# Softmax divisors spread by repeating loads instead of widening matmuls, and GpSimd's scatter moved to the head of its step

## Chip, cores and metric

The kernel runs on one core of a Trainium2 chip. The metric is the device time of one execution in microseconds, here the median of three. TensorE's clock has two levels, 1.2 and 2.4 GHz; a granted clock of 1.00 is the upper one and 0.50 the lower one.

## The reference, cut to what matters

Four sequences of 512 tokens with 512 channels go through a gated cross attention (32 query heads in 8 groups, 16 channels each, causal) and a gated mixture of experts:

```python
x = x + tanh(g_xattn[0]) * xattn(layernorm(x), ctx, ctx, mask, w_q, w_k, w_v, w_o, b_o)
x = x + tanh(g_ffn[0]) * ffn(layernorm(x), Wg, W1, W3, W2, Ws1, Ws3, Ws2)
```

Inside `xattn` each head's output is a softmax-weighted sum of values, divided by the sum of its weights, and all heads together are then projected with `w_o` and the bias `b_o`. Inside `ffn` a shared expert is applied to all tokens, and each token also goes to 4 of 16 experts, whose results are added with the router's weights.

## The kernel before

The kernel is five stages, each a block whose engines wait for each other at its end: `stage_project` (layer norm, queries, keys, values), `stage_attend`, `stage_close` (normalising the heads, output projection, residual, second layer norm, router scores), `stage_shared` (shared expert and routing tables) and `stage_experts` (79 tiles of 128 token slots).

**Attention** handles 32 items (a sequence and a group of four heads). For each it writes an unnormalised output of 128 rows to DRAM (`do`): each head has 16 channels and 16 copies of its softmax sum. SP's program (L586 to L606) is written out in order: loads for later items, the row of maxima, the store of the item before (L584), and in item 28 the loads of the sums of sequences 0 to 2 and of sequence 0's channels. ScalarE's copy of an item into `a_o` waits until the store before has landed. After the last maximum VectorE splits the bias into three bf16 parts (L656 to L671), and then takes the reciprocal of the 96 rows of sums (L674) and rounds it into a high and a low part (L676, L678).

**The closing stage** needs, for each channel and token, the inverse of that head's sum. It has one row per head. TensorE widens it with a selecting matrix `pick` (L977): two matmuls (high and low part) per quarter of the channels into the PSUM tiles `c_den`, and VectorE multiplies the channels by them (L931). The whole order of TensorE's work is in L1031 to L1054: 16 token tiles, four per sequence; for each a projection (`project`, one matmul for the bias at L985 and eight at L987 into a ring of RING = 3 banks), then the widening for the next sequence's quarter, and from the ninth tile on a transpose of a normalised tile (`turn`, L1000), eight tiles behind. VectorE does in each tile the scaled addition of the residual (L946), the statistics (L949) and then the multiply for the next sequence; after four tiles it finishes the deviation (L954, L115 to L127) and normalises (L963). A sequence's first projection waits until all four of its multiplies are done. SP loads the last sequence's sums, then the channels of sequence 1, the gate's scalar `gx`, the shared expert's weights and the channels of sequences 2 and 3. ScalarE takes the tanh of the scalar (L844), and the scaled additions wait for it. GpSimd subtracts high parts from the weights to get their low parts (L886, L890), and stores the normalised tokens.

**The experts.** In every tile TensorE makes gate and up products in three passes, turns the hidden row tile, multiplies down in three passes (L1706), and the third of these needs the low part of the hidden tile. GpSimd's step (L1587 to L1598) makes the low part of the tile before (`low_h`, L1582), the product of gate and up (L1593), then issues the scatter-add of the results two tiles back (L1577) and a gather four tiles ahead (L105). A scatter waits for ScalarE's result (L1624) and for the landing of the scatter before it. After the last tile GpSimd makes one more low part and issues the last two scatters.

Of the kernel before, what the change touches and what calls it, by code (L numbers as in the profile page):

```python
# [16 lines left out]
P = 128  # L17
# [125 lines left out]

def context(io, b):
# [80 lines left out]
def stage_project(nc, io, dram):  # L225

    SPIN, SEAM = 48, 48
    with ExitStack() as c:  # L228
# [15 lines left out]
        pick, less = sb("p_pick", [P, KD * P]), sb("p_less", [P, P])  # L244
# [60 lines left out]
        def _(eng):  # L305
            begin(eng, s_eps, s_ones, s_fill, s_mask, s_warm, io["s_pick"])
# [16 lines left out]
            eng.memset(pick[:], 0.0).then_inc(s_fill, 1)  # L323
# [7 lines left out]
            eng.wait_ge(s_fill, 6)  # L331
# [6 lines left out]
            eng.wait_ge(s_mask, BATCH + 4)  # L338
            eng.tensor_copy(io["lessr"], less[:]).then_inc(io["s_pick"], 1)
            eng.tensor_copy(io["pick"], pick[:]).then_inc(io["s_pick"], 1)  # L340
# [4 lines left out]
            eng.wait_ge(s_fill, 8)  # L345
# [174 lines left out]
def stage_attend(nc, io, dram):  # L520
# [3 lines left out]
    with ExitStack() as c:  # L524
# [45 lines left out]
        def _(eng):  # L570
# [15 lines left out]
            for i in range(NIT):  # L586
# [56 lines left out]
        def _(eng):  # L643
            begin(eng, s_split, io["s_triple"], io["s_inv"])
# [10 lines left out]

            eng.memset(three, 0.0).then_inc(s_split, 1)  # L656
# [15 lines left out]
            eng.wait_ge(io["s_sums"], 16)  # L672
            most = slice(0, (BATCH - 1) * GROUPS * HG)
            eng.reciprocal(inv[most], sums[most]).then_inc(s_split, 1)  # L674
            eng.wait_ge(s_split, 7)
# [91 lines left out]
def stage_close(nc, io, dram):  # L767
# [4 lines left out]
    with ExitStack() as c:  # L772
# [152 lines left out]
        def _(eng):  # L925
# [7 lines left out]
            for k in range(KD):  # L933
                normalise(0, k)
# [876 lines left out]
```

## Time and profile before

| what | us |
|---|---|
| median of 3 runs (lowest, highest) | 1240.26 (1237.85, 1240.94) |
| the profiled execution | 1240.24 |
| its span, first to last instruction | 1238.2 |
| TensorE busy, matmuls | 1199.9 (97%) |
| VectorE, ScalarE, GpSimd busy | 636.2, 576.4, 626.3 |
| closing stage, first matmul to end of the block | 359.9 to 461 |
| experts, about | 675 to the end |

Times inside the kernel are microseconds from the span's first instruction. In a timeline row the first number is the start, the second the length; several instructions in a row are merged ("x4"), and the bracket tells how long the engine had been idle and what ended that. The profiled execution's time lies 2.0 us above its span, which is what lies around the instructions.

### The profile page before, as it was taken

What the parts mean: (1) busy time and instruction counts of PE and PEld (TensorE: products, weight loads), DVE (VectorE), ACT (ScalarE), POOL (GpSimd) and SP (SyncE); (2) the same over time, 40 slices, a digit from 0 to 9 for tenths busy, and PEclk for the clock granted to TensorE, in tenths of its full rate; (3) what the DMA queues carried; (4) which work ended last, traced back from release to release, by engine and by line L of the source; (5) the groups of instructions that cost most, each with busy time, mean ns of one, the idle gap of its engine ahead of it and who ended that gap; (6) DMA issues with size and microseconds to landing.
All of it is one profiled execution on the core that took longest, in us unless ns stands there. A gap on an engine that the chain in (4) does not pass through costs nothing. (4 is left out here: it accounts for less than half of the span.)

```text
span 1238.2 us, 23635 instructions
## 1 busy us (share of the span) xinstructions
PE 1199.9 (97%) x7811; PEld 919.4 (74%) x7812; DVE 636.2 (51%) x1832; ACT 576.4 (47%) x990; POOL 626.3 (51%) x662
## 2 busy tenths in 40 slices
PE   7999999999999989999998999999999999999994
PEld 5564555555543458888887999999999999999994
DVE  5337999999965658865142133322523444542100
ACT  1221777777742234322332554555554554555552
POOL 7010333433334124635562666666666667767663
PEclk8999999999989999999999999999999999999997
DMA  9462544444545050100133455665655666665433
GB/s 348 149 189 99 154 125 131 126 135 126 145 134 155 30 204 17 52 35 35 51 121 113 107 102 144 142 150 138 155 138 129 163 147 146 142 150 138 83 61 42
DMA packets 73965, 153.27 MB, mean 124 GB/s; under 512 B 10740, under 2 KB 16372, under 8 KB 73128
## 3 DMA queue, kind: packets, MB, share of 16 engines
q1 hardware_dynamic: 52856, 102.50, 25.6%
q0 software_dynamic: 21040, 49.88, 19.5%
q8 instruction: 41, 0.67, 0.2%
q14 instruction: 28, 0.23, 0.1%
HBM read 97.69 MB, written 52.23 MB: 121 GB/s over the span
## 5 line engine op out<-in xcount | busy, mean ns | idle before, releaser
L1553 DVE CAST e_w<-e_w 128x480 fp32r<-128x480 f32 x135 | 75.7, 561 | 303.9 <-DMA e_w<-in_w2T 299.7
L653 DVE CUSTOM_DVE_ANT_0 a_mb<-a_mb,late 128x512 f32<-128x512 f32 (+1 forms) x480 | 217.3, 527 | 6.3 <-PE a_mb L696 4.6
L1706 PE MATMUL e_yps<-e_w,e_hT 128*128 x711 | 197.2, 404 | 0.9 <-ACT e_hT L1616 0.9
L639 ACT ACTIVATE a_at<-a_eb 128x1024 f32<-128x1024 f32 (+1 forms) x192 | 163.4, 869 | 38.5 <-PE a_eb L717 25.7
L566 POOL TENSOR_SCALAR_AFFINE_SELECT a_at<-a_at 128x256 f32<-128x256 f32 (+1 forms) x192 | 94.2, 491 | 170.6 <-ACT a_at L639 170.6
L1685 PE MATMUL e_up<-e_w,e_xT 128*128 x948 | 170.4, 328 | 0.0
L1685 PE MATMUL e_gate<-e_w,e_xT 128*128 x948 | 169.2, 327 | 1.0 <-issue 1.0
L1685 PEld LDWEIGHTS e_gate<-e_w,e_xT 128*128 128x128 f32 x948 | 157.2, 190 | 11.4 <-issue 6.6
L1685 PEld LDWEIGHTS e_up<-e_w,e_xT 128*128 128x128 f32 x948 | 149.4, 188 | 0.0
L1706 PEld LDWEIGHTS e_yps<-e_w,e_hT 128*128 128x128 f32 x711 | 128.1, 189 | 25.4 <-issue 1.2
L1577 POOL DMA_INDIRECT out<-e_y,scatter x79 | 128.3, 1625 | 25.3 <-issue 14.1
L1582 POOL TENSOR_TENSOR e_hT<-e_hc,e_hT 128x384 fp32r<-128x384 f32 x79 | 85.6, 1083 | 108.4 <-ACT e_hc L1617 108.4
L696 PE MATMUL a_mb<-a_k,a_q 49*128 49x512 f32 (+1 forms) x480 | 132.4, 373 | 0.8 <-PEq L228 0.8
L696 PEld LDWEIGHTS a_mb<-a_k,a_q 49*128 49x128 f32 x480 | 74.2, 184 | 65.5 <-DVE a_mx L653 39.2
L1560 DVE TENSOR_TENSOR e_w<-e_w 128x480 fp32r<-128x480 f32 x135 | 101.6, 753 | 4.7
L740 PE MATMUL a_pv<-a_at,a_v 128*32 128x128 f32 (+1 forms) x1792 | 102.2, 327 | 0.2
L1593 POOL TENSOR_TENSOR e_h<-e_act,e_upc 128x352 f32<-128x352 f32 x79 | 79.5, 1006 | 38.4 <-ACT e_upc L1635 37.3
L105 POOL DMA_INDIRECT e_x<-dx,gather x79 | 82.6, 1046 | 23.6 <-issue 23.5
L1612 ACT ACTIVATE e_xT<-e_xps 128x512 fp32r<-128x512 f32 x79 | 47.2, 597 | 81.5 <-PE e_xps L1676 76.3
L717 PE MATMUL a_eb<-a_q,a_k 50*128 50x512 f32 (+1 forms) x256 | 84.1, 420 | 0.1
L1631 ACT ACTIVATE e_act<-e_gate 128x352 f32<-128x352 f32 x79 | 36.7, 464 | 95.8 <-PE e_gate L1685 95.8
L1635 ACT ACTIVATE e_upc<-e_up 128x352 f32<-128x352 f32 x79 | 36.8, 466 | 79.0 <-PE e_up L1685 79.0
(265 smaller groups left out, 1873.7 us busy)
## 6 DMA issues: line engine op xcount, KB each, us to landing
e_w<-in_w13T SPq DMA_DIRECT2D x16, 1408.0 KB
dq<-p_parts SPq DMA_DIRECT2D x32, 256.0 KB, 2.4
a_q<-dq SPq DMA_DIRECT2D x64, 128.0 KB
do<-a_o SPq DMA_DIRECT2D x32, 256.0 KB, 2.3
e_w<-in_w2T SPq DMA_DIRECT2D x16, 512.0 KB
a_k<-dk SPq DMA_DIRECT2D x64, 98.0 KB
e_w<-in_ctxT SPq DMA_DIRECT2D x4, 1024.0 KB, 14.1
e_w<-in_x SPq DMA_DIRECT2D x4, 1024.0 KB, 13.5
```

The lines of the kernel that those rows point to most:

```text
L105: eng.indirect_dma_start(out=io["rows"][n], out_offset=None, in_=dram["x2"], in_offset=bass.IndirectOffsetOnAxis(ap=io["gather"][:, g:g + ...
L566: eng.affine_select(out=square, in_=square, compare_op=ALU.is_ge, fill=0.0, base=0, pattern=[[0, 2 * len(js)], [1, P]], channel_multiplier ...
L639: eng.activation(to, scores, ACT.Exp, scale=0.25).then_inc(s_exp, 1)
L653: eng.tensor_tensor_reduce(out=b[:, 0:w], in0=b[:, 0:w], in1=io["late"][:, SEQ - w:SEQ], scale=1.0, scalar=3 * NEG, op0=ALU.add, op1=ALU.m ...
L696: mm = eng.matmul(b, q[r][rows, j, ch * P:(ch + 1) * P], k[r][rows, 0:b.shape[-1]], start=True, stop=True)
L717: return eng.matmul(eb[u % 2][:, t, n0:SEQ], keys, q[r][rows, js[0], n0:SEQ], start=True, stop=True)
L740: mm = eng.matmul(pv[32 * h:32 * h + 32, cols], v[of % NB][:, ch, :], at[of % 2][:, ch, 2 * j + t, cols], start=ch == 0 and n0 == 0, stop= ...
L1560: eng.tensor_tensor(w[rows, r, rest], w[rows, r, rest].bitcast(F32), w[rows, r, cols].bitcast(F32), ALU.subtract).then_inc(s_low, 1)
L1577: eng.indirect_dma_start(out=out, out_offset=bass.IndirectOffsetOnAxis(ap=io["scatter"][:, g:g + 1], axis=0), in_=y[n][:], in_offset=None, ...
L1582: eng.tensor_tensor(hT[r][:, 1], hc[:], hT[r][:, 0].bitcast(F32), ALU.subtract).then_inc(s_hlow, 1)
L1685: mm = eng.matmul(out[r][:], xT[r][:, mine, k, :], w[:, bass.ds(buf, 1), its * SIDE + at:its * SIDE + at + INTER].rearrange("p b n -> p (b ...
L1706: mm = eng.matmul(yps[:], hT[r][0:size, mine, n, :], w[0:size, bass.ds(buf, 1), its * SIDE + at:its * SIDE + at + D].rearrange("p b n -> p ...
```

## The change

The divisors are no longer widened on TensorE. VectorE's reciprocal of the first three sequences is taken straight after the last maximum; SP stores it to a DRAM tensor `dinv`, one DMA per sequence, in the last item but one, and in the last item waits for these stores and loads sequence 0's rows back, repeated over the 16 channels of every head (1 MB to 128 partitions). VectorE's four multiplies for sequence 0 move into the attention block. In the closing stage SP loads the scalar first, then the channels of sequence 1 and its repeated inverse, and so on; the last sequence's inverse makes its trip to DRAM in that stage, and its repeated rows come in two pieces. Both operands of the multiply now lie in SBUF. The multiply for the next sequence comes first in VectorE's tile instead of last; the ring of banks has five members. The matrix `pick` and the high and low parts of the inverse are gone. In the experts the scatter moves to the head of GpSimd's step, and the last tile's low part is made by VectorE straight from PSUM.

```diff
+def store_inverse(eng, dram, b, tile, done):
+    heads = tile[b * GROUPS * HG:(b + 1) * GROUPS * HG]
+    eng.dma_start(dram["inv"][b].rearrange("r (k n) -> k r n", k=KD), heads).then_inc(done, 16)
+
+def load_inverse(eng, dram, b, k0, k1, tile, done):
+    src = dram["inv"][b:b + 1, :, k0 * SEQ:k1 * SEQ].broadcast_to([HD, 2 * HG, (k1 - k0) * SEQ])
+    eng.dma_start(tile.rearrange("p k n -> p (k n)"), src).then_inc(done, 16)
+
+def normalise(eng, io, o, inv, k):
+    eng.tensor_tensor(o[:, k], o[:, k], inv, ALU.mult).then_inc(io["s_on"], 1)
...
@@ stage_project, gpsimd @@
-            for b in range(BATCH):
-                mine = pick[b * GROUPS * HG:(b + 1) * GROUPS * HG].rearrange("p (k w h) -> p k w h", k=KD, w=HD)
-                eng.affine_select(out=mine, in_=mine, compare_op=ALU.not_equal, fill=1.0, base=0,
-                                  pattern=[[-2 * HG, KD], [0, HD], [-1, 2 * HG]], channel_multiplier=1).then_inc(s_mask, 1)
...
@@ stage_attend, sync @@
+                if i == NIT - 1:
+                    eng.wait_ge(io["s_sums"], 16 * BATCH)
+                    load_inverse(eng, dram, 0, 0, KD, io["inv"], io["s_heads"])
                 if i:
                     store(i - 1)
...
+                if i == NIT - 2:
+                    eng.wait_ge(io["s_inv"], 2)
+                    for b in range(BATCH - 1):
+                        store_inverse(eng, dram, b, inv, io["s_sums"])
@@ stage_attend, vector @@
+            most = slice(0, (BATCH - 1) * GROUPS * HG)
+            eng.wait_ge(io["s_sums"], 16)
+            eng.reciprocal(inv[most], sums[most]).then_inc(io["s_inv"], 1)
             eng.memset(three, 0.0).then_inc(s_split, 1)
...
-            eng.tensor_copy(io["inv"][most, 0], inv[most]).then_inc(io["s_inv"], 1)
-            eng.wait_ge(io["s_inv"], 2)
-            eng.tensor_tensor(io["inv"][most, 1], inv[most], io["inv"][most, 0].bitcast(F32), ALU.subtract).then_inc(io["s_inv"], 1)
+            eng.wait_ge(io["s_heads"], 16 * (KD + 1))
+            for n in range(KD):
+                normalise(eng, io, io["heads"], io["inv"][:, n], n)
@@ stage_close, sync @@
-    RING, LAG, SEAM = 3, 8, 24
+    RING, LAG, SEAM = 5, 8, 24
...
+            eng.dma_start(gx[:], io["gx"].broadcast_to([P, 1])).then_inc(s_g, 16)
+            load_heads(eng, dram, 1, o[1], s_o[1])
+            load_inverse(eng, dram, 1, 0, KD, x2[0][:], s_o[1])
             load_sums(eng, dram, BATCH - 1, BATCH, sums, io["s_sums"])
...
             for b in range(2, BATCH):
                 load_heads(eng, dram, b, o[b], s_o[b])
+            load_inverse(eng, dram, 2, 0, KD, x2[1][:], s_o[2])
+            eng.wait_ge(io["s_inv"], 3)
+            store_inverse(eng, dram, BATCH - 1, inv, io["s_sums"])
+            eng.wait_ge(io["s_sums"], 16 * (BATCH + 2))
+            load_inverse(eng, dram, BATCH - 1, 0, KD - 1, rest[:], s_o[BATCH - 1])
...
@@ stage_close, vector @@
+                    if b + 1 < BATCH:
+                        divide(b + 1, j)
+                    if i == 1:
+                        eng.wait_ge(io["s_sums"], 16 * (BATCH + 1))
+                        eng.reciprocal(inv[LAST], sums[LAST]).then_inc(io["s_inv"], 1)
                     eng.wait_ge(s_op, i + 2)
...
                     eng.bn_stats(stats[:, j, :], x1[b][:, j]).then_inc(s_st, 1)
-                    if b + 1 < BATCH:
-                        normalise(b + 1, j)
@@ stage_close, tensor @@
-            for k in range(KD):
-                widen(0, k)
...
                     project(b, j)
-                    if b + 1 < BATCH:
-                        widen(b + 1, j)
@@ stage_experts, gpsimd @@
+                if g >= 2:
+                    scatter(g - 2)
                 if g:
                     low_h(g - 1, 1 - r)
...
-                if g >= 2:
-                    scatter(g - 2)
...
-            low_h(LAST, LAST % 2)
             scatter(LAST - 1)
             scatter(LAST)
@@ stage_experts, vector @@
+            high, rest = hT[LAST % 2][:, 0], hT[LAST % 2][:, 1]
+            eng.wait_ge(s_hT, 2 * LAST + 2)
+            eng.tensor_tensor(rest, hps[:], high.bitcast(F32), ALU.subtract).then_inc(s_hlow, 1)
@@ stage_experts, scalar @@
-                eng.activation(hc[:], hps[:], ACT.Copy).then_inc(s_hT, 1)
+                if not isinstance(g, int) or g < LAST:
+                    eng.activation(hc[:], hps[:], ACT.Copy).then_inc(s_hT, 1)
```

## Rows read from the trace of the kernel before

**Rows 1.** Timeline, end of attention and head of the closing stage
```profile
343.13 0.11 DVE L656 MEMSET k_three<- 96x64 uint32 x1
...
346.88 9.90 SPq L584 DMA_DIRECT2D do<-a_o  x3
...
359.87 1.16 PE L977 MATMUL c_den<-k_inv,k_pick 32*128 32x512 f32 x4 [1.20 <-PEq L524]
...
364.12 3.35 DVE L936 RECIPROCAL e_w<-e_w 32x512 f32<-32x512 f32 x1
...
364.24 0.59 PE L985 MATMUL c_op<-k_triple,k_three 96*128 96x512 bf16 x1 [0.87 <-DVE e_w L931]
...
367.37 0.20 ACT L844 ACTIVATE c_tg<-c_gx 128x1 f32<-128x1 f32 x1 [10.93 <-DMA c_gx<-in_gx]
...
371.02 0.69 DVE L949 BATCH_NORM_STATS2 c_stats<-e_w 128x6 f32<-128x512 f32 x1
```

**Rows 2.** Timeline, first matmul of sequences 1 to 3, last scaled addition
```profile
385.51 0.61 PE L985 MATMUL c_op<-k_triple,k_three 96*128 96x512 bf16 x1 [1.51 <-DVE c_o L931]
...
406.40 0.39 PE L985 MATMUL c_op<-k_triple,k_three 96*128 96x512 bf16 x1 [1.50 <-DVE c_o L931]
...
427.08 0.39 PE L985 MATMUL c_op<-k_triple,k_three 96*128 96x512 bf16 x1 [0.91 <-DVE c_o L931]
...
445.12 0.75 DVE L946 SCALAR_TENSOR_TENSOR e_w<-c_op,c_tg,e_w 128x512 f32<-128x512 f32 x1 [2.17 <-PE c_op L987]
```

**Rows 3.** Timeline, steps of one token tile with and without widening
```profile
395.34 0.73 PE L977 MATMUL c_den<-k_inv,k_pick 32*128 32x512 f32 x2
...
399.75 0.73 PE L977 MATMUL c_den<-k_inv,k_pick 32*128 32x512 f32 x2
...
437.18 0.38 PE L985 MATMUL c_op<-k_triple,k_three 96*128 96x512 bf16 x1
...
441.27 0.38 PE L985 MATMUL c_op<-k_triple,k_three 96*128 96x512 bf16 x1
```

**Rows 4.** Timeline, the last scatters and the last result but one
```profile
1219.34 1.58 POOL L1577 DMA_INDIRECT out<-e_y,scatter  x1 [0.15 <-issue]
...
1219.81 0.69 ACT L1624 ACTIVATE e_y<-e_yps,scale 128x512 f32<-128x512 f32 x1 [1.63 <-PE e_yps L1706]
...
1224.73 1.56 POOL L1577 DMA_INDIRECT out<-e_y,scatter  x1 [2.38 <-ACT e_y L1624]
1230.29 1.56 POOL L1577 DMA_INDIRECT out<-e_y,scatter  x1 [4.00 <-DMA out<-e_y,scatter]
```

**Rows 5.** DMA issues of the span: size of one, median us to landing
```profile
do<-a_o SPq DMA_DIRECT2D x32, 256.0 KB, 2.3
...
out<-e_y,scatter POOLq DMA_INDIRECT x79, 4.9
...
e_w<-in_bo SPq DMA_DIRECT2D x1, 256.0 KB, 3.6
```

**Rows 6.** Windows: PE, PEld, DVE, ACT, POOL busy (count), granted clock, DMA share, GB/s
```profile
127.00:128.00 1.00, 1.00 (x12) 0.46 (x11) 0.76 (x3) 0.79 (x1) 0.15 (x1) 1.00 0.87 240
...
386.00:387.00 1.00, 1.00 (x3) 0.48 (x2) 0.82 (x7) 0.07 (x1) 0.00 (x0) 0.50 1.03 387
```

**Rows 7.** Lines L931 and L1560 (min/median/max ns), and timeline of L963
```profile
L931 DVE TENSOR_TENSOR c_o<-c_o,c_den x12: 669/670/672, 371.6 to 426.4; 128x512 f32<-128x512 f32 x12
...
L1560 DVE TENSOR_TENSOR e_w<-e_w x135: 657/659/1434, 675.2 to 1149.1; 128x480 fp32r<-128x480 f32 x120, 96x512 fp32r<-96x512 f32 x15
...
432.15 6.66 DVE L963 TENSOR_SCALAR c_x<-e_w,c_mv,c_rstd 128x512 f32<-128x512 f32 x4
```

**Rows 8.** Timeline, one tile of the experts on GpSimd, ScalarE and TensorE
```profile
897.79 1.06 POOL L1593 TENSOR_TENSOR e_h<-e_act,e_upc 128x352 f32<-128x352 f32 x1 [0.26 <-ACT e_upc L1635]
...
900.10 0.69 ACT L1624 ACTIVATE e_y<-e_yps,scale 128x512 f32<-128x512 f32 x1 [0.18 <-PE e_yps L1706]
...
903.25 1.01 POOL L1582 TENSOR_TENSOR e_hT<-e_hc,e_hT 128x384 fp32r<-128x384 f32 x1 [1.35 <-ACT e_hc L1617]
...
905.84 0.64 PEld L1706 LDWEIGHTS e_yps<-e_w,e_hT 128*128 128x128 f32 x3
```

More of the change, by code:

```diff
@@ L243, in stage_project @@
         const = sb("p_const", [1, 2, SEQ])
-        pick, less = sb("p_pick", [P, KD * P]), sb("p_less", [P, P])
+        less = sb("p_less", [P, P])
         proj = [ps(f"p_proj{i}", [P, SEQ]) for i in range(KD + 1)]
@@ L789, in stage_close @@
         wraw = sb("c_wraw", [P, GATE])
+        assert GATE - UP == SEQ
         stats, mv, rstd = sb("c_stats", [P, CH, 6]), sb("c_mv", [P, CH, 2]), sb("c_rstd", [P, CH])
         root, work, eps = sb("c_root", [P, CH]), sb("c_work", [P, CH]), sb("c_eps", [P, 1])
-        den = [ps(f"c_den{i}", [P, SEQ]) for i in range(2)]
+        rest = sb("c_inv", [P, KD - 1, SEQ])
         op = [ps(f"c_op{i}", [P, D]) for i in range(RING)]
@@ L800, in stage_close @@
         s_tg, s_eps = sem("c_stg"), sem("c_seps")
-        s_den, s_on, s_op, s_x1, s_st, s_mv, s_root, s_newton, s_x2 = (
-            sem(f"c_s{n}") for n in ("den", "on", "op", "x1", "st", "mv", "root", "newton", "x2"))
+        s_op, s_x1, s_st, s_mv, s_root, s_newton, s_x2 = (
+            sem(f"c_s{n}") for n in ("op", "x1", "st", "mv", "root", "newton", "x2"))
         s_tr, s_xT, s_lg, s_lc, s_whigh, s_wlow = (sem(f"c_s{n}") for n in ("tr", "xT", "lg", "lc", "whigh", "wlow"))
@@ L805, in stage_close @@
         weights = shared_weights(io)
+        spread = [None, [x2[0][:, n] for n in range(KD)], [x2[1][:, n] for n in range(KD)], [rest[:, n] for n in range(KD - 1)] + [wraw[:, UP:]]]
         block = c.enter_context(nc.Block())
@@ L925, in _, with divide @@
         def _(eng):
[L926 to L927 removed]
+            begin(eng, s_x1, s_st, s_mv, s_newton, s_x2)
+            def divide(b, k):
                 if k == 0:
[L929 to L940 removed]
+                    eng.wait_ge(s_o[b], 16 * (KD + (1 if b < BATCH - 1 else 2)))
+                normalise(eng, io, o[b], spread[b][k], k)
             eng.wait_ge(s_tg, 2)
@@ L967, in _ @@
         def _(eng):
-            begin(eng, s_den, s_op, s_tr, s_lg, s_part)
-            def widen(b, k):
-                d = b * KD + k
-                if d >= 2:
-                    eng.wait_ge(s_on, d)
-                rows = slice(b * GROUPS * HG, (b + 1) * GROUPS * HG)
-                if b == BATCH - 1 and k == 0:
-                    eng.wait_ge(io["s_inv"], 6)
-                for part in range(2):
-                    mm = eng.matmul(den[k % 2][:], io["pick"][rows, k * P:(k + 1) * P], io["inv"][rows, part], start=part == 0, stop=part == 1)
-                mm.then_inc(s_den, 1)
+            begin(eng, s_op, s_tr, s_lg, s_part)
             def project(b, j):
                 i = b * CH + j
-                eng.wait_ge(s_on, (b + 1) * KD + 1)
+                eng.wait_ge(io["s_on"], (b + 1) * KD + 1)
                 if i >= RING:
@@ L1029, in score @@
                     mm.then_inc(s_lg, 1)
-            eng.wait_ge(io["s_pick"], 3)
-            eng.wait_ge(io["s_inv"], 3)
-            for k in range(KD):
-                widen(0, k)
             eng.wait_ge(io["s_wo"], 16 * (KD + 2))
@@ L1051, in _ @@
                     score(BATCH - 1, i - (NT + LAG - CH + 2))
-            eng.wait_ge(s_on, BATCH * KD + 1)
+            eng.wait_ge(s_x1, NT + 1)
             for _ in range(SEAM):
-                eng.matmul(den[0][:, 0:P], io["onesb"], io["before"], start=True, stop=True)
+                eng.matmul(op[0][:, 0:P], io["onesb"], io["before"], start=True, stop=True)
 def stage_shared(nc, io, dram, out):
```

37 lines of the change are left out of this document (9 added, 28 removed).

## The prediction

> **What bounds the kernel now.** I read the page first: TensorE is busy nearly throughout, so time is gained only where it waits or does work that can go. The chain of waits ends in the experts' matmuls and, at the very end, in scatters. The timeline at the seam of attention and closing stage [rows 1] then shows four widening matmuls at 359.87, VectorE multiplying their results, and TensorE's first projection only at 364.24. The start of each later batch [rows 2] shows TensorE waiting for VectorE's multiply: 1.51 us at 385.51, 1.50 at 406.40, 0.91 at 427.08; a batch takes 20.9, 20.7 and 18.0 us (the last has no widening beside it). A step of one token tile [rows 3] takes 4.41 us with its two widening matmuls (0.73), and 4.09 without them but with a turn (437.18 to 441.27). So TensorE bounds this stage, with VectorE close behind. At the kernel's end [rows 4] the last scatters follow each other at 5.4 and 5.6 us (1219.34, 1224.73, 1230.29), though the result of the last tile but one is ready at 1220.5: each scatter waits for the one before to land (the row of 1224.73 names ScalarE's result, but that had been there for 4 us).
>
> **Attention's end.** The reciprocal of three batches' sums moves up to 343.1, straight behind the last maximum, and takes 3.35 us (by the row at 364.12, of as many columns), so it is done when SP has put the store of 346.88 in its queue [rows 1]. The bias's split slides behind it and is hidden: TensorE needs it at 360. The two rounding operations go too; they were hidden. SP then issues three stores of the inverse (1.5 us), waits for them, and loads 1 MB that repeats rows. A store lands 2.3 us after its issue [rows 5]. What a load that repeats rows costs, the trace shows only for the bias, one row over 128 partitions: 240 GB/s at a DMA share of 0.87, or 276 at full share; plain loads move 387 [rows 6]. I take 276 as the nearest kind: 3.8 us for 1 MB. The bounds are 2.7 us (387 GB/s) and, if all of the bias load's 3.6 us from issue to landing [rows 5] was transfer, 4 x 3.6 = 14.4. So the store lands at 350.7, the load at 350.7 + 3.8 + 1.6 = 356.1 (the 1.6 is a store's 2.3 less its own movement), and four multiplies of 0.67 end at 358.8. Behind SP's wait are the stores of the last two head groups; the last but one now queues behind 1 MB, and ScalarE's last copy waits for its landing. I charge 0.5 us for both to the block's end.
>
> **First batch of the closing stage.** The eight widening matmuls at its head are gone and the projections start at 360.4, but that gain isn't kept: VectorE's new first work is the multiply of batch 1, which waits for 1 MB of heads and 1 MB of inverse. Heads and the gate's scalar, in the old order, have landed at 367.37 [rows 1]; in the new order the same two come the other way round. Add 0.5 and 3.8: 371.7. Then VectorE does four multiplies (0.67), three scaled additions (0.75, row 445.12) and three statistics (0.69), and the last batch's reciprocal (3.35; SP, and so the last inverse, waits on it): 2.7 + 2.2 + 2.1 + 3.4 = 10.4, and 0.6 for the port (below). Batch 1 starts at 382.7 instead of 385.5: **2.8 us**. TensorE is through its four tiles by 377 and waits. The five banks in place of three are worth next to nothing here: three tiles last until 373.2, and the first scaled addition frees a bank at 373.1. Loading the scalar first is costed at nothing, since tanh at 367.37 is hidden behind the projection, which ends at 370.
>
> **Batch 1.** Today: four steps of 4.41, the end wait of 1.50, and 20.89 - 17.64 - 1.50 = 1.75 us more because the clock is at its lower level after the wait (0.50 at 386 [rows 6]). The wait remains and so does, I assume, the slow start. New: 4 x 3.68 + 1.75 = 16.5. **4.4 us**. The end wait goes because each multiply now stands ahead of its step, not behind it. **Batch 2:** 20.69 becomes 4 x 4.09 = 16.4: **4.3 us**. **Batch 3** is as it was, less 0.5 us that I charge for VectorE being late with its four multiplies: its second normalisation meets GpSimd's weights. The last batch's divisors should be there: 9 MB queued from 359.4 at 276 GB/s end at 393, the store and reload of 64 KB and its piece make about 397, and they are wanted at 406. Sum for the stage: 2.8 + 4.4 + 4.3 - 0.5 = **11.0 us**. What follows, to the stage's end, hangs on the last projection as now.
>
> **The port.** Sixteen multiplies now read both operands from SBUF. With one from PSUM they took 669 to 672 ns whatever GpSimd did; the experts' subtraction with both in SBUF takes 657 ns but up to 1434, and at 432.15 four normalisations took 6.66 us beside GpSimd's splitting [rows 7]. The Trainium skill, "SBUF — State Buffer", section "Who interferes with whom", says a VectorE instruction with two SBUF inputs contends with a GpSimd one that reads SBUF, which speaks against this change; these rows agree. In the sum stand 0.6 us in batch 0 and 0.5 in batch 3.
>
> **Experts.** Scatter(g-2) goes from the end of GpSimd's step to its head. In a step [rows 8] the product before ends at 898.85, the gather that follows it 1.3 later at 900.15, its result is there at 900.79, so the scatter runs to about 902.5, ahead of the low part's 903.25. TensorE wants that part only at 905.84, 1.6 us after its end. So nothing per tile; 2.3 us is the slack before a tile gets longer. At the end the scatter of the last tile but two starts 5 us earlier and has landed by 1220, so the next starts at 1220.6 when its result is ready, and the last at about 1226.1 instead of 1230.29 (a landing is 4.9 [rows 5], 5.5 between two here): **4.2 us**. The last low part on VectorE and ScalarE's copy saved are worth nothing: the chain is the landings. The mask that selected channels goes from GpSimd's first microseconds, hidden under the input loads: nothing.
>
> **Sum.** 11.0 + 4.2 = 15.2. The profiled execution took 1240.24 us around a span of 1238.2, and the median is 1240.26: 1225.0 us. A measurement of this kernel tells 0.3% (3.7 us) from no change.
>
> **Rivals.**
> *Loads at half rate or less.* For: 16 copies of the same rows are read at once; no row shows it. Against: the bias row. At 7.6 us per MB the seam and batch 1's start lose 3.8 each and batch 2 some more: 1233. Chance 0.12.
> *The port decides.* If every multiply beside GpSimd waits a whole splitting operation (6.66 / 4 - 0.54 = 1.1 us more each), two in batch 0 and four in batch 3 lie on the path: 6.6 in place of 1.1, so 1230. The skill's rule would give this time. Against: GpSimd splits weights only in some stretches. Chance 0.13.
> *Better than forecast.* The load runs at 387 GB/s twice (2.2 us), the clock stays up through the wait (1.75), VectorE isn't late (1.1): 1220. For: after the waits at 406.40 and 427.08 the bias's matmul took 0.39 us, against 0.61 at 385.51 [rows 2]. Chance 0.15.
> *Slower than before.* Repeated rows come at a rate that makes the four loads the bound. All four lie ahead of batch 3, which at 3.8 us per MB could start at 397 + 6.7 = 403.7 for all that the loads demand (6.7: four multiplies with three steps between), and later by 4 x (L - 3.8) for L us per MB; with the scatter's 4.2 it breaks even at L = 10.7 and is over 0.3% slower from 11.6. At 14.4 it is 1255. Chance 0.03.
> *The scatter at the head holds the step.* If the previous scatter lands over 2.3 us late, TensorE waits in each of 77 tiles; 0.2 us each eats the whole gain: 1240. Against: a landing takes 4.9 of 7 us. Chance 0.03.
> The forecast itself has 0.54. Faster 0.94, same 0.03, slower 0.03. The range takes the better case's 1219 and goes up to 1232.
>
> **What would show it.** No widening; first projection near 360.4; VectorE's first multiply of the stage ending a wait for a load at 371 to 372; batch starts near 383, 399, 416; the last scaled addition near 434 instead of 445.12; last scatter near its predecessor plus 5.5, both 4 us nearer to the last result. It is wrong if the block of attention closes over 2 us later, if batch 2 or 3 waits for a load, or if a tile of the experts takes longer than now.

## The result and the profile after

The changed kernel took 1230.77 us in the median of 4 runs (1229.68 to 1231.72), the kernel before 1240.60 beside it (4 runs, 1237.85 to 1241.05): a ratio of 0.9929, with a 95% interval of 0.9910 to 0.9947. That is 9.8 us less, where 15.2 had been forecast; the direction and the range were right, the size was not. The profiled execution has a span of 1227.9 us against 1238.2.

Six distances between landmarks show where the time went. They are differences of starts in the timelines, for two profiles of each kernel (the second ones are the runs e12 and e11 below):

| from, to | before | before, again | after | after, again |
|---|---|---|---|---|
| attention's first matmul (from the span's start) | 119.33 | 119.22 | 118.34 | 118.36 |
| to the closing stage's first matmul | 240.54 | 240.60 | 243.16 | 243.46 |
| attention's first matmul to the last scaled addition | 325.79 | 325.87 | 317.53 | 317.58 |
| last scaled addition to the experts' first matmul | 221.28 | 223.84 | 225.51 | 225.44 |
| that to ScalarE's last result `e_y` | 557.02 | 557.17 | 556.59 | 556.72 |
| last `e_y` to the last scatter | 6.87 | 7.02 | 2.44 | 2.96 |

So attention and closing stage together gave 8.3 us, the scatters 4.1 to 4.4, and between them the span loses 1.6 to 4.2 us in a part that the change hardly touches. The experts' tiles are 0.4 us shorter in sum. The 1.0 us ahead of attention came with a shorter stretch at the lower clock in the first stage (19.0 to 26.5 us in place of 16.5 to 27.5, read in windows of half a microsecond). It is not the change's own: attention starts at 118.79 in e1 below, which has the first stage of the kernel before, and at 119.60 and 119.19 in e2 and e7, which have that of the changed kernel.

**The seam.** SP's queue at the end of attention, in the timeline of the changed kernel:

```profile
346.27 1.94 SPq L147 DMA_DIRECT2D dinv<-a_inv  x3
350.15 0.57 SPq L153 DMA_DIRECT2D e_w<-dinv  x1
351.41 7.20 SPq L594 DMA_DIRECT2D do<-a_o  x2
...
360.73 0.34 SPq L828 DMA_DIRECT2D c_gx<-in_gx  x1
```

the first of SP's loads in the next stage in the kernel before,

```profile
358.94 0.32 SPq L141 DMA_DIRECT2D e_w<-do  x1
```

and what VectorE and ScalarE do in the changed kernel:

```profile
357.00 2.49 DVE L158 TENSOR_TENSOR e_w<-e_w 128x512 f32<-128x512 f32 x4 [6.37 <-DMA e_w<-dinv]
...
357.66 0.60 ACT L637 ACTIVATE a_o<-a_pv 128x512 f32<-128x512 f32 x1 [4.17 <-DMA do<-a_o]
...
374.02 0.69 DVE L158 TENSOR_TENSOR c_o<-c_o,c_x 128x512 f32<-128x512 f32 x1 [14.52 <-DMA c_x<-dinv]
...
376.73 3.35 DVE L965 RECIPROCAL e_w<-e_w 32x512 f32<-32x512 f32 x1
...
383.48 0.94 DVE L158 TENSOR_TENSOR c_o<-c_o,c_x 128x512 f32<-128x512 f32 x1
```

The megabyte of repeated rows is issued at 350.15 and VectorE goes on at 357.00: 6.8 us, where I had 5.4. The store of the last item but one (351.41) stands in the same queue behind it, and ScalarE's last copy waits 4.17 us for its landing. The last store goes out only then, and SP is in the next stage at 360.73, where the kernel before had been at 358.94. With the 1.0 us from ahead of attention that is 2.8 us late (3.1 in e11 against e12); I had charged 0.5. The store did not wait in idle queues: in windows of half a microsecond the DMA engines move 1.33 MB between 351.5 and 357.0, which is the megabyte and the 256 KB of the store together, and nothing in the 2 us behind.

**The batches.** The starts of sequences 0 to 3 on TensorE, and the last scaled addition, which answer to [rows 1, 2]:

```profile
361.50 0.59 PE L993 MATMUL c_op<-k_triple,k_three 96*128 96x512 bf16 x1 [3.83 <-PEq L534]
...
384.48 0.61 PE L993 MATMUL c_op<-k_triple,k_three 96*128 96x512 bf16 x1 [5.30 <-DVE c_o L158]
...
400.77 0.38 PE L993 MATMUL c_op<-k_triple,k_three 96*128 96x512 bf16 x1
...
417.83 0.39 PE L993 MATMUL c_op<-k_triple,k_three 96*128 96x512 bf16 x1 [0.54 <-DVE c_o L158]
...
435.87 0.75 DVE L967 SCALAR_TENSOR_TENSOR e_w<-c_op,c_tg,e_w 128x512 f32<-128x512 f32 x1 [1.80 <-PE c_op L995]
```

Batch 1 starts 1.03 us earlier than before (nearly all of it the shift from ahead of attention), lasts 16.29 us in place of 20.89, batch 2 lasts 17.06 in place of 20.68, batch 3 18.04 as before. 1.03 + 4.60 + 3.62 = 9.25 us.

**The tail of the stage** is where time was lost again. TensorE's last scores, the matmuls at the seam and the first of the shared expert, changed kernel:

```profile
447.52 3.50 PE L1035 MATMUL c_lp<-e_w 128*128 128x16 f32 x24
450.86 2.72 PE L1056 MATMUL c_op<-before,onesb 128*128 128x128 bf16 x24
455.06 7.85 PE L1405 MATMUL s_gate<-s_xT,s_ws 128*128 x24 [1.48 <-issue]
```

and the same three in the kernel before:

```profile
456.77 2.75 PE L1027 MATMUL c_lp<-e_w 128*128 128x16 f32 x24
459.37 1.50 PE L1054 MATMUL c_den<-before,onesb 128*128 128x128 bf16 x24
462.27 5.73 PE L1403 MATMUL s_gate<-s_xT,s_ws 128*128 x24 [1.39 <-issue]
```

The work is the same; 0.75 + 1.22 + 2.12 = 4.1 us of difference. The windows of the changed kernel (columns as in [rows 6]) show the granted clock at its lower level there:

```profile
446.00:449.00 3.00, 3.00 (x29) 2.87 (x27) 0.00 (x0) 1.21 (x3) 0.00 (x0) 1.00 0.87 362
449.00:452.00 3.00, 3.00 (x24) 3.00 (x24) 0.00 (x0) 0.22 (x1) 0.00 (x0) 0.55 0.85 341
452.00:455.00 3.00, 1.58 (x15) 1.31 (x13) 0.06 (x1) 0.62 (x1) 0.65 (x5) 0.50 0.04 14
455.00:458.00 3.00, 2.94 (x7) 2.37 (x8) 2.21 (x10) 1.75 (x4) 0.00 (x0) 0.50 0.03 3
```

That of the kernel before is 1.00 throughout:

```profile
445.00:470.00 25.00, 21.02 (x159) 17.09 (x158) 12.11 (x49) 12.51 (x23) 4.09 (x10) 1.00 0.53 211
```

**The end of the kernel**, which answers to [rows 4]:

```profile
1211.33 1.01 POOL L1587 TENSOR_TENSOR e_hT<-e_hc,e_hT 128x384 fp32r<-128x384 f32 x1 [0.71 <-ACT e_hc L1622]
...
1215.31 1.56 POOL L1582 DMA_INDIRECT out<-e_y,scatter  x1 [1.58 <-ACT e_y L1629]
...
1217.97 0.69 ACT L1629 ACTIVATE e_y<-e_yps,scale 128x512 f32<-128x512 f32 x1 [2.56 <-PE e_yps L1711]
...
1220.41 1.57 POOL L1582 DMA_INDIRECT out<-e_y,scatter  x1 [3.54 <-DMA out<-e_y,scatter]
```

The last scatter but one goes out as soon as its result is there, and the last follows it by 5.1 us: it waits for the landing.

### The profile page after: what moved, and what is told of

Read it like the earlier page. It is cut to its first block and busy times, and to the rows that moved or that the text cites. A ratio compares the mean times of both kernels' runs of the same rounds, so it can differ in the third digit from the quotient of the medians.

```text
span 1227.9 us, 23555 instructions
## 1 busy us (share of the span) xinstructions
PE 1190.7 (97%) x7779; PEld 917.2 (75%) x7780; DVE 631.8 (51%) x1829; ACT 576.0 (47%) x989; POOL 618.1 (50%) x655
## 5 line engine op out<-in xcount | busy, mean ns | idle before, releaser
L1555 DVE CAST e_w<-e_w 128x480 fp32r<-128x480 f32 x135 | 71.5, 530 | 304.9 <-DMA e_w<-in_w2T 300.8
L1600 POOL TENSOR_TENSOR e_h<-e_act,e_upc 128x352 f32<-128x352 f32 x79 | 76.3, 966 | 39.7 <-ACT e_upc L1640 39.5
```

## The experiments

Twelve kernels ran. Those of one group shared a chip and the runs of the kernel before: e1 to e4 (13 runs of the kernel before, 1241.30 us in the median), e5 to e8 (21 runs, 1241.12) and e9 to e12 (13 runs, 1240.52). Since the chips differ, variants are compared by their ratio to the kernel before; that of the change is 0.9929 in its first comparison and 0.9936 in e11.

**e1, the scatter at the head alone**, in the kernel before, with the last low part left on GpSimd:

```diff
@@ kernel before, stage_experts, gpsimd @@
+                if g >= 2:
+                    scatter(g - 2)
                 if g:
                     low_h(g - 1, 1 - r)
...
-                if g >= 2:
-                    scatter(g - 2)
```

> The kernel before with nothing but the scatter moved to the head of GpSimd's step; the last low part stays on GpSimd. Theory A (landings chain the last scatters; order inside a tile costs nothing): all of the end's gain comes from this one move, the last scatter starts about 2.4 us behind the last result instead of 6.9, 1240.6 - 4.4 = 1236.2 us, and a tile stays at 6.98 us. Rival B (the low part on VectorE and the copy saved carry part of it, or tiles get longer at the head's wait): gain under 2.5 us, 1238 or more.

1238.32 us (10 runs), ratio 0.9974 (0.9959 to 0.9989). GpSimd at the end:

```profile
1223.22 1.01 POOL L1582 TENSOR_TENSOR e_hT<-e_hc,e_hT 128x384 fp32r<-128x384 f32 x1 [2.15 <-ACT e_hc L1617]
1224.39 1.56 POOL L1577 DMA_INDIRECT out<-e_y,scatter  x1 [0.16 <-issue]
1229.97 1.57 POOL L1577 DMA_INDIRECT out<-e_y,scatter  x1 [4.02 <-DMA out<-e_y,scatter]
```

The result of the last tile but one is there at 1222.39, and its scatter goes out at 1224.39: it stands behind the last low part on GpSimd, which waited 2.15 us for ScalarE. The last scatter comes 4.64 us behind the last result: 2.2 of the 6.87 are gone, not 4.2. The other 2.2 (4.64 against 2.44) is then the last low part's move to VectorE, with the copy that it saves ScalarE, which I had called worth nothing; no kernel with that move alone was run. No tile became longer (experts 556.96 us against 557.02).

**e2, the closing stage's part alone** (the changed kernel with the experts' edits undone: scatter behind the product, last low part on GpSimd, ScalarE's last copy back).

```diff
@@ changed kernel, stage_experts, gpsimd @@
-                if g >= 2:
-                    scatter(g - 2)
                 if g:
                     low_h(g - 1, 1 - r)
...
+                if g >= 2:
+                    scatter(g - 2)
...
+            low_h(LAST, LAST % 2)
             scatter(LAST - 1)
             scatter(LAST)
```

> The changed kernel with the experts' part of the kernel before (scatter behind the product, last low part on GpSimd). Theory A: the divisors' part alone is worth 1240.6 - 1230.8 - 4.4 = 5.4 us, so 1235.2 us. Rival B (the two parts do not add up, because what happens after the closing stage depends on when it ends): 1233 or less, or 1237 or more.

1233.33 us (1233.03 to 1235.87), ratio 0.9937 (0.9920 to 0.9954), between theory A's 1235.2 and rival B's 1233. The last scatter is again 6.49 us behind the last result, the stretch from attention to the last scaled addition 317.96. So the two halves are about 8 and 3 us on the medians; their sum, 11, is within what these medians leave open of the 9.8. The tail, from the last scaled addition to the experts, was 225.46 us here, as in both profiles of the whole change.

**e3, what the repetition costs.** The loads of the inverse read 8 KB rows of the tokens, as many bytes to the same places; the output is not the reference's.

```diff
@@ load_inverse @@
-    src = dram["inv"][b:b + 1, :, k0 * SEQ:k1 * SEQ].broadcast_to([HD, 2 * HG, (k1 - k0) * SEQ])
+    src = dram["plain"][b * SEQ:(b + 1) * SEQ].rearrange("(p a) d -> p (a d)", p=P)[:, k0 * SEQ:k1 * SEQ]
```

> The changed kernel, but each load of the repeated inverse reads as many bytes of the input tokens, one contiguous row of 8 KB per partition; so the division by the softmax sums is replaced by a product with tokens, and the routing is another. Only the closing stage is compared. Theory A (reading the same rows sixteen times costs transfer time): the first load lands in 5.4 us or less after its issue instead of 6.8, attention's block closes 1 to 1.5 us earlier, and batch 1 starts at 381 to 382 instead of 384.5. Rival B (a megabyte behind stores and heads takes this long whatever it reads): 6.8 within 0.3, batch 1 at 384 to 385.

1223.44 us in the one run. Theory A holds in its direction (batch 1 at 381.36), with a first load of 5.8 us where it said 5.4 or less. The landing times of the changed kernel's loads (issue to landing is the last column):

```profile
c_x<-dinv SPq DMA_DIRECT2D x2, 1024.0 KB, 13.6
e_w<-dinv SPq DMA_DIRECT2D x1, 1024.0 KB, 6.8
c_inv<-dinv SPq DMA_DIRECT2D x1, 768.0 KB, 5.6
```

and in e3 the same loads, with VectorE's first multiply and TensorE's batch 1:

```profile
c_x<-in_x SPq DMA_DIRECT2D x2, 1024.0 KB, 11.3
c_inv<-in_x SPq DMA_DIRECT2D x1, 768.0 KB, 4.5
```

```profile
356.26 2.50 DVE L158 TENSOR_TENSOR e_w<-e_w 128x512 f32<-128x512 f32 x4 [5.31 <-DMA e_w<-in_x]
...
381.36 0.39 PE L993 MATMUL c_op<-k_triple,k_three 96*128 96x512 bf16 x1 [2.67 <-DVE c_o L158]
```

Repeated rows cost 1.0 to 1.1 us per load more than plain ones of the same size (6.8 against 5.8, 5.6 against 4.5), and 2.3 in the median of the two that share the queue with the channels. The edit changes two things at once, the repetition and the tensor that is read (rows stored a few microseconds ago against input); which of them costs is not separated. Attention's first matmul lies 0.3 us later here. Batch 1 starts 3.1 us earlier, its first matmul takes 0.39 us and no longer 0.61, and the stretch to the last scaled addition is 312.85 in place of 317.53. So of the 4.7 us that the repeated loads cost 3.4 lie ahead of batch 1 (262.75 from attention's first matmul against 266.14) and the other 1.3 are about what the lower clock cost in that batch, which in e3 stays away (16.29 us in the changed kernel, 14.6 for four steps of 3.65). All this rests on one run.

**e4, more work for TensorE in the tail**: six matmuls of 128 columns, written to a spare bank, behind each of the last four scores.

```diff
@@ stage_close, tensor @@
                     score(BATCH - 1, i - (NT + LAG - CH + 2))
+                    for _ in range(FILL):
+                        eng.matmul(op[1][:, 0:P], io["onesb"], io["before"], start=True, stop=True)
```

> The changed kernel with six 128-column bf16 matmuls into a free bank after each of the last four groups of score matmuls, 24 in all, about 1.4 us of TensorE. Theory A (the lower clock level that the changed kernel has from 449.3 to 459.2 came because TensorE did little in the last score matmuls of 16 columns, and it costs 4.2 us): the granted clock stays at 1.00 over the seam, 1230.8 - 4.2 + 1.4 = 1228 us. Rival B (the drop comes whatever TensorE does there): the clock still falls and the time is 1232.

1227.92 us (1226.77 to 1230.68), ratio 0.9900 (0.9879 to 0.9921). The lower level is there for about 3.5 us, from 450.2, and not for 10 (449.2 to 459.5):

```profile
449.00:452.00 3.00, 3.00 (x36) 3.00 (x34) 0.00 (x0) 0.22 (x1) 0.00 (x0) 0.71 0.62 254
452.00:455.00 3.00, 1.61 (x12) 1.26 (x11) 0.60 (x4) 1.27 (x1) 0.65 (x5) 0.72 0.03 3
455.00:458.00 3.00, 3.00 (x15) 2.46 (x14) 2.28 (x8) 1.74 (x4) 0.00 (x0) 1.00 0.01 0
```

From the last scaled addition to the experts it took 223.82 us in place of 225.5. Of the 2.3 us by which this profile's span is shorter than that of the change, 0.8 lie ahead of attention and 1.2 in attention, which the edit does not touch, so the lead does not show what the edit is worth. Theory A's time came, but not its reason in full: the clock still falls. Its interval overlaps that of the change itself (0.9910 to 0.9947); e10 puts the same matmuls to a second test.

**e5, the last sequence's reciprocal later**, ahead of the fourth scaled addition and not the second, so that batch 1's multiplies do not stand behind it.

```diff
@@ stage_close, vector @@
-                    if i == 1:
+                    if i == CH - 1:
                         eng.wait_ge(io["s_sums"], 16 * (BATCH + 1))
```

> The changed kernel with the last sequence's reciprocal (3.35 us) moved in VectorE's program from behind the second multiply for batch 1 to behind the fourth. Theory A (VectorE's chain of four multiplies, three additions, three statistics and this reciprocal sets the start of batch 1, and the last inverse has 6 us of slack, since its store queues behind loads until 388 in any case): batch 1 starts 3.3 us earlier, at 381.1 instead of 384.5, and the kernel takes 1230.8 - 3.3 = 1227.5 us. Rival B (the last inverse is as late as batch 1): batch 1 starts earlier but batch 3 waits for its divisors, and the time stays within 1 us.

1235.85 us (11 runs), ratio 0.9958 (0.9943 to 0.9974): by the ratios some 3 us slower than the changed kernel. Batch 1 started at 380.26, 4.2 us earlier, as meant, and with a wait of 0.88. But batch 3 began at 422.08. VectorE and GpSimd in e5, and TensorE's start of batch 3:

```profile
403.79 0.18 DVE L115 RECIPROCAL c_rstd<-c_root 128x4 f32<-128x4 f32 x1 [4.57 <-ACT c_root L873]
...
416.98 4.50 POOL L925 TENSOR_TENSOR s_xT<-c_x2T,s_xT 128x2048 fp32r<-128x2048 f32 x1 [5.32 <-ACT s_xT L892]
417.74 4.28 DVE L158 TENSOR_TENSOR c_o<-c_o,c_wraw 128x512 f32<-128x512 f32 x1
...
422.08 0.61 PE L993 MATMUL c_op<-k_triple,k_three 96*128 96x512 bf16 x1 [6.38 <-DVE c_o L158]
```

VectorE, early now, waits 4.57 us for a square root that ScalarE has queued behind rounding weights still on their way (they land at 400.7). And its fourth multiply of batch 2 meets GpSimd's 4.50 us subtraction, which had started 0.76 us earlier: 4.28 us in place of 0.67. The Trainium skill, "SBUF — State Buffer", section "Who interferes with whom", says that a VectorE instruction with two SBUF inputs contends with a GpSimd one that reads SBUF, and that the port pair they share is an exclusive lock. These rows agree: the multiply ends 0.54 us behind the subtraction (422.02 against 421.48), about its own length of 0.67. The changed kernel itself escaped this by little: there the fourth multiply starts at 417.10 and GpSimd's subtraction at 418.57.

**e6, sequence 0's inverse with a semaphore of its own**, stored and loaded ahead of the stores of the other two.

```diff
@@ stage_attend, sync @@
-                if i == NIT - 1:
-                    eng.wait_ge(io["s_sums"], 16 * BATCH)
-                    load_inverse(eng, dram, 0, 0, KD, io["inv"], io["s_heads"])
...
-                    for b in range(BATCH - 1):
-                        store_inverse(eng, dram, b, inv, io["s_sums"])
+                    store_inverse(eng, dram, 0, inv, io["s_first"])
+                    eng.wait_ge(io["s_first"], 16)
+                    load_inverse(eng, dram, 0, 0, KD, io["inv"], io["s_heads"])
+                    for b in range(1, BATCH - 1):
+                        store_inverse(eng, dram, b, inv, io["s_sums"])
...
```

> The changed kernel, but sequence 0's inverse is stored first with a semaphore of its own, and its repeated rows are loaded as soon as that one store has landed, before the other two stores are issued. Theory A (the close of attention's block is late because the megabyte of repeated rows lies in the queues ahead of the store of the last group but one, whose landing ScalarE's last copy waits for): the load is issued 1.3 us earlier, the block closes 1.3 us earlier, 1229.5 us. Rival B (the first batch of the closing stage waits for the landing of its own two megabytes and the time hidden there returns): the block closes earlier and batch 1 starts no more than 0.3 us earlier.

1231.21 us (1228.84 to 1238.18), ratio 0.9928 (0.9902 to 0.9954): nothing. The multiply came at 356.68, 1.0 us nearer to attention's start, but the closing stage still began 243.30 us behind it (243.16 and 243.46 without the edit). So VectorE's multiplies do not close the block; the last stores do, of which ScalarE's copy waits for the first to land:

```profile
352.20 7.16 SPq L594 DMA_DIRECT2D do<-a_o  x2
...
358.41 0.60 ACT L638 ACTIVATE a_o<-a_pv 128x512 f32<-128x512 f32 x1 [4.12 <-DMA do<-a_o]
```

But theory A failed too. The megabyte is issued 1.2 us nearer to attention's start, and the store behind it, issued when its data is there as before, still takes 6.2 us to the copy (358.41 against 352.20; 6.25 in the changed kernel, 5.4 in e3; the median store of this kernel lands in 2.3 [rows 5]). So what holds the store is the traffic that it meets, and an earlier start of the load does not shorten it; why is not shown. In the profiled execution the port collision of e5 happened here too (4.86 us for the fourth multiply, beside a subtraction of 4.49 that started 0.19 us earlier), and batch 3 waited 6.38 us.

**e7, the multiply behind its step again**, as it was before the change:

```diff
@@ stage_close, vector @@
-                    if b + 1 < BATCH:
-                        divide(b + 1, j)
...
                     eng.bn_stats(stats[:, j, :], x1[b][:, j]).then_inc(s_st, 1)
+                    if b + 1 < BATCH:
+                        divide(b + 1, j)
```

> The changed kernel with VectorE's multiply for the next sequence behind the statistics of its tile, as in the kernel before. Theory A (the head of the step is what removes TensorE's waits at batches 2 and 3): the waits of 1.5 us at the starts of batches 2 and 3 return, batch 1 starts about where it does now or up to 1 us later, 1230.8 + 3 = 1233.8 us. Rival B (with five banks TensorE's lead hides it): within 1 us of 1230.8.

1234.40 us (9 runs), ratio 0.9953 (0.9933 to 0.9974): by the ratios 2 to 3 us slower than the change, and 3.1 in the profile (320.67 us from attention's first matmul to the last scaled addition, in place of 317.53). The waits are back, against none and 0.54 us:

```profile
403.56 0.39 PE L993 MATMUL c_op<-k_triple,k_three 96*128 96x512 bf16 x1 [2.17 <-DVE c_o L158]
...
421.82 0.39 PE L993 MATMUL c_op<-k_triple,k_three 96*128 96x512 bf16 x1 [1.73 <-DVE c_o L158]
```

**e8, three banks and the gate's scalar behind the inverse**, as in the old order:

```diff
@@ stage_close @@
-    RING, LAG, SEAM = 5, 8, 24
+    RING, LAG, SEAM = 3, 8, 24
...
-            eng.dma_start(gx[:], io["gx"].broadcast_to([P, 1])).then_inc(s_g, 16)
             load_heads(eng, dram, 1, o[1], s_o[1])
             load_inverse(eng, dram, 1, 0, KD, x2[0][:], s_o[1])
             load_sums(eng, dram, BATCH - 1, BATCH, sums, io["s_sums"])
+            eng.dma_start(gx[:], io["gx"].broadcast_to([P, 1])).then_inc(s_g, 16)
```

> The changed kernel with three banks instead of five and the gate's scalar loaded behind the channels and the inverse of sequence 1. Theory A (neither is worth anything: the first scaled addition waits for the megabyte of inverse in any case): within 1 us of 1230.8. Rival B (with three banks TensorE stops for the fourth tile until the first addition, and again while VectorE takes the reciprocal; or tanh comes behind the multiply): 1232 or more, the fourth projection starting after 375 instead of 375.4 or the first addition after 375.

1227.84 us (1225.46 to 1232.83), ratio 0.9908 (0.9880 to 0.9935), below what either theory gave. Neither edit is worth anything; that they cost something is not shown, since the intervals overlap and of this profile's lead of 4.2 us 1.5 lie ahead of attention and 1.4 in it, which the edit does not touch. From the closing stage's first matmul to the last scaled addition it took 73.96 us, against 74.37 and 74.12 in the two profiles of the change.

**e9 and e10, a version meant to beat the change**: e5's later reciprocal, ScalarE's second square root ahead of rounding the shared down projection, and GpSimd's subtraction held until the multiplies are done; e10 with e4's matmuls as well.

```diff
@@ on top of e5: stage_close, scalar and gpsimd @@
             deviation(0)
+            deviation(1)
             high_weights(2)
...
-                if b + 1 < BATCH:
+                if 0 < b and b + 1 < BATCH:
                     deviation(b + 1)
...
                     eng.wait_ge(s_xhigh, CH + 1)
+                    eng.wait_ge(io["s_on"], BATCH * KD + 1)
                     eng.tensor_tensor(xT[:, 1], x2T[0], xT[:, 0].bitcast(F32), ALU.subtract).then_inc(s_wlow, 1)
```

> The changed kernel with three edits: VectorE takes the last sequence's reciprocal ahead of the fourth scaled addition, not the second (as in the run e5); ScalarE takes the second batch's square root ahead of rounding the experts' shared down projection, which waits for a load; and GpSimd's subtraction of the first batch's transposed operand (4.5 us, two SBUF operands) waits until VectorE has done all its multiplies. Theory A (what spoiled e5 was VectorE's 4.57 us wait for that square root and the 4.28 us multiply beside GpSimd's subtraction; both go here): batch 1 starts near 380.5, no multiply of batch 3 takes over 1.5 us, batch 3 starts near 414 with a wait under 1.5 us in place of 6.38, last scaled addition near 432; median near 1227.5 (1225 to 1230). Rival B (VectorE's own work between the batches is what is late): batch 3 still waits 3 us or more though every multiply takes 0.7 us, last addition 435 or later, 1230 or more.

> As e9, with e4's 24 extra matmuls of 128 columns among the last scores (they write a spare bank and change no value). Theory A (the gains add: e4 gave 2.9 us on the median of the changed kernel, through a shorter stretch at the lower clock in the tail): 1225 (1222 to 1228), and the lower level at the seam to the shared stage lasts under 7 us. Rival B (the lower level comes elsewhere then, or is as long whatever the tail does): within 1 us of e9, with 10 us at the lower level after the last projection.

e9 took 1233.01 us (ratio 0.9927, 0.9910 to 0.9944), e10 1232.74 (0.9947, 0.9924 to 0.9970), the changed kernel beside them 1232.23. No gain. In e9 batch 1 starts at 381.12, and the wait for the square root is 0.36 us; but batch 3 waits 4.08:

```profile
403.58 6.73 POOL L912 TENSOR_TENSOR e_w<-e_w 128x512 fp32r<-128x512 f32 x5 [14.63 <-ACT e_w L865]
...
404.26 0.48 DVE L979 MEMSET e_w<- 64x512 f32 x1 [2.10 <-ACT e_w L866]
404.78 5.82 DVE L984 TENSOR_SCALAR c_x<-e_w,c_mv,c_rstd 128x512 f32<-128x512 f32 x4
410.52 1.75 DVE L158 TENSOR_TENSOR c_o<-c_o,c_inv 128x512 f32<-128x512 f32 x1
...
418.27 0.39 PE L995 MATMUL c_op<-k_triple,k_three 96*128 96x512 bf16 x1 [4.08 <-DVE c_o L158]
```

VectorE's next instruction, clearing the padding rows of those weights, waits 2.10 us for the same rounding; then four normalisations take 5.82 us beside GpSimd's splitting, where the first batch's took 1.91, and the multiply behind them 1.75. So the normalisation behind batch 1 is tied to when the down projection arrives (ScalarE's rounding starts on its landing, at 400.04 in the changed kernel, 400.71 in e5 and 401.17 in e9): an earlier batch 1 only waits there. Theory A had named one of the two waits on that load, and rival B's forecast of the wait (3 us or more) came, though not its condition that every multiply takes 0.7 us. In e10 the tail was at the lower level from 448.4 to 458.6 in spite of the extra matmuls, and they then took time themselves (227.48 us from the last scaled addition to the experts, 227.07 in e9 without them): e4's short stretch does not repeat.

**e11 and e12, both kernels again**, for a second profile of each.

> The changed kernel again, unchanged, as the baseline of e9 and e10 on the same chip and as a second profile of it. Theory A (the lower clock of 449 to 460 in the first profile is usual for this kernel, since two of the variants with the same tail showed it): median 1230.8 within 1 us, a stretch of 7 us or more at the lower level between the last projection and the shared stage's matmuls, shared stage's matmuls over 6 us for the first 36. Rival B (it was that execution's own): no such stretch, profiled span under 1225.

> The kernel before again, unchanged, for a second profile of it. Theory A (the kernel before has in most executions no stretch at the lower level in the tail, which is why the change gave 4 us back there): span near 1238, the shared stage's first matmul 17.1 to 17.3 us behind the last scaled addition and no stretch between 445 and 475. Rival B (where such stretches fall differs between executions of either kernel alike): a stretch of 3 to 10 us in the tail here as well, and then about 1240 to 1242 in the span.

e11: 1232.23 us (1227.83 to 1237.61), ratio 0.9936 (0.9911 to 0.9960), and the lower level from 448.5 to 459 as in the first profile. e12: 1243.08 us in its one run. Its batches start at 385.44, 404.67 and 427.05, and in its tail:

```profile
455.00:460.00 5.00, 5.00 (x52) 4.87 (x52) 0.00 (x0) 1.64 (x4) 0.00 (x0) 1.00 0.92 375
460.00:465.00 5.00, 3.52 (x22) 2.77 (x19) 1.85 (x8) 1.56 (x3) 0.70 (x5) 0.54 0.21 77
```

The kernel before has such a stretch too, in this profile and in e1's (460 to 467, 459.7 to 466.5), shorter and later than the changed kernel's. Rival B's two numbers came, a stretch of 7 us and a span of 1241.0; that both kernels are alike is not shown. Of the 4.2 us that the first two profiles showed, 1.6 remain against these two (225.5 against 223.85), and 2.5 against the mean of the three (222.99).

All the profiles together tell more. The tails without extra matmuls, by how long the lower level lasts in them:

| lower level in the tail, about | runs | last scaled addition to the experts |
|---|---|---|
| none | before | 221.28 |
| 3.5 us | e3 | 222.86 |
| 7 us | e12, e1 (kernel before), e6 (change) | 223.84, 223.86, 223.89 |
| 10 us | after, e11, e2, e7, e8 | 225.51, 225.44, 225.46, 225.42, 225.46 |
| 13.5 us | e5, e9 | 227.06, 227.07 |

e6 runs the changed kernel's tail and takes as long as the kernel before with a stretch as long. So the loss is the clock's and not that of the changed instructions; what makes the stretch 10 us in five profiles with the change and at most 7 in three of the kernel before stays open.

The same holds inside the stage: in e12 and e1 the slow start is not that of batch 1 but of batch 2 (in e12 batch 1 lasts 19.23 us and batch 2 22.38, against 20.89 and 20.68 in the first profile).

## Why the prediction was right in sign and too large

By its own steps, in the order of the prediction:

- **Attention's end: the term was too small, and this is a step that failed.** "Load lands 356.1" was 357.0, and "I charge 0.5 us" measured 2.8 to 3.1, beyond the 2 us that the prediction gives as a sign of being wrong. The mechanism was named (a store behind 1 MB, ScalarE's copy waiting for it) but not worked out: the store takes 6.2 us and not 2.3, ScalarE copies only then, and the last store follows. e6 shows that this chain and not VectorE closes the block; e3, with a plain load, gets back 0.8 of it.
- **The price of repetition was right, the rest of the load was not.** At 276 GB/s in place of 387 the sum charges 1.1 us for it, and e3 measures 1.0 to 1.1. But the plain megabyte takes 5.8 us from issue to reader, where the sum's terms (2.7 of movement and 1.6) make 4.3: no term stood for the 256 KB store that moves beside it, which at 276 GB/s is an estimated 0.9 of the missing 1.5 us. That the bias row, repeated 128 times, gave the right price for 16 copies is in part luck.
- **Batch 1's start: 2.8 us forecast, none found** (1.03, which is the shift from ahead of attention). The first multiply came at 374.0 and not at 371.7, and with that shift it is 3.3 us late: 2.3 for the later block, 1.0 for the loads. From there to batch 1 it took 10.5 us where the sum had 11.0. The reciprocal in the midst of them is a real 3.4 us (e5: 380.26), but taking it out buys nothing, since the next thing on VectorE then waits for weights.
- **Batch 1: 4.4 forecast, 4.6 measured**, the slow start kept as assumed (0.61 us for the bias matmul). **Batch 2: 4.3 forecast, 3.6 measured**, because the 0.5 us of VectorE being late, charged to batch 3, falls at batch 2's end (0.54). e7 shows that it is the multiply's place ahead of its step that takes the waits away. How well the two batches fit one by one is luck of the execution: against e12 they give 2.9 and 5.3 us, with the same sum.
- **"What follows hangs on the last projection as now": wrong by 1.6 to 4.2 us**, and this is the largest miss beside batch 1's start. The same matmuls ran at the lower clock for longer (e11 again). Why the stretch begins 13 us behind the last scaled addition in the changed kernel and 15 or not at all in the other is not settled: it begins 15 us behind in e6 too, which has the changed tail; e4 shortened it once, e10 did not.
- **The port: 0.6 us for batch 0 was 0.3** (the multiply of 0.94 us), and batch 3's 0.54 (1.06 in e11) follows the second batch's normalisations, 4.95 us in the changed kernel beside GpSimd's splitting against 1.91 for the first batch of e9, without it. As a rival it did not decide here, but by luck of order: e5 and e6 show it at 4.3 and 4.9 us for one multiply, 3.6 and 4.2 us over 0.67, where that rival had charged 1.1 for one.
- **The scatters: 4.2 forecast, 4.1 to 4.4 measured, one reason wrong.** Half of it is the place at the head (e1), the other half, by difference, the last low part's move to VectorE. The prediction looked at the chain of landings and not at what stood ahead of the last scatter but one on GpSimd.
- **Banks, the scalar's order, the mask: nothing**, as costed (e8, for the first two).

The sum by what was measured: 8.3 - 2.5 (against the mean of three profiles) + 4.3, up to 0.4 in the experts' tiles, and 0.4 to 1.0 from ahead of attention, is 10.5 to 11.5; the medians say 9.8 in the first comparison and 8.3 in the last. The difference is not accounted for; single profiles of one kernel differ by 2.8 us in span here (1238.2 and 1241.0).

## What to carry to other kernels

When a big load goes into a queue near the end of a stage, follow what stands behind it in that queue to the end of the stage; the small store behind it landed no earlier than the megabyte in any profile here. Moving divisors from matmuls to loads pays where TensorE is the bound (0.73 us a step here), but makes the multiply one with two SBUF operands, and then a single long GpSimd instruction in the wrong microsecond costs more than all the small effects together: read on the trace how near the two come. Before a loss is put down to a change, compare the granted clock in the same stretch over several profiles of both kernels. And when an engine is made earlier, look for the next instruction in its own order that waits for data, before the gain is counted.

## What the hardware showed unexpectedly

A load of 1 MB whose source repeats each row 16 times took 6.8 us from issue to its reader, a plain one from another tensor 5.8 (768 KB, from issue to landing: 5.6 and 4.5). A VectorE multiply of 128x512 with both operands in SBUF took 4.28 and 4.86 us in place of 0.67 when a GpSimd subtraction of 4.5 us had started 0.76 or 0.19 us before it; the one that started 1.47 us ahead of such a subtraction took 0.67. And a stretch at TensorE's lower level in the same place of the same program differs between executions and between neighbours in code: none or 7 us for the kernel before, 10 twice for the changed one, 7 in e6 with the same tail, 3.5 or 10 with the same extra matmuls. The stage's tail grows with it, from 221.3 to 227.1 us.
